# Scan products of two units in one TensorE run, and decays masked by GpSimd selects

## What is computed

```python
xBC = jax.nn.silu(conv)                       # 4 taps over time
dt_p = jax.nn.softplus(dt + dt_bias)
A = -jnp.exp(A_log)
dA = jnp.exp(dt_p * A)
dtx = dt_p[..., None] * x
def step(state, inp):
    dA_t, dtx_t, B_t, C_t = inp
    state = state * dA_t[..., None, None] + dtx_t[..., None] * B_t[:, :, None, :]
    y_t = jnp.einsum('bhpn,bhn->bhp', state, C_t)
    return (state, y_t)
...
yn = (yg * lax.rsqrt(var + EPS)).reshape(B, L, I) * norm_weight
yn = yn * jax.nn.silu(gate)
```

## Time and profile before

| | |
|---|---|
| median of 3 runs | 3058.53 us (3056.78 to 3059.67) |
| profiled execution | 3058.11 us, span 3056.6 us |
| TensorE busy | 3001.3 us, 98% of the span |
| VectorE busy | 2137.6 us, 70% |
| ScalarE busy | 1750.5 us, 57% |
| GpSimd busy | 678.0 us, 22% |
| mean granted TensorE clock | 0.997 |

### The profile page before, as it was taken

One profiled execution on the slowest core, in us unless ns is written; L12 is line 12 of the kernel. 1 busy time (PEld: TensorE's weight loads), 2 busy tenths in 40 slices (PEclk: granted clock), 3 DMA queues, 4 the chain that ended last, 5 costly groups with the idle time before them and its releaser, 6 DMA issues.

```text
span 3056.6 us, 45099 instructions
## 1 busy us (share of the span) xinstructions
PE 3001.3 (98%) x14304; PEld 2339.3 (77%) x14304; DVE 2137.6 (70%) x2660; ACT 1750.5 (57%) x3716; POOL 678.0 (22%) x543
## 2 busy tenths in 40 slices
PE   7999999999999998999999999999999999999998
PEld 6777777777777777777777777777776888887787
DVE  7767666676666676767666666766667878677877
ACT  3576575757566575576665757575665232234443
POOL 3322223121212234312222231212124000001112
PEclk9999999999999999999999999999999999999999
DMA  3434343343425353434243433434254444456665
GB/s 130 165 132 150 104 159 122 137 141 107 158 92 173 104 185 120 157 121 168 98 167 104 157 123 136 140 110 159 92 173 151 145 141 148 144 197 210 212 209 182
DMA packets 125528, 444.86 MB, mean 146 GB/s; under 512 B 17488, under 2 KB 21712, under 8 KB 109008
## 3 DMA queue, kind: packets, MB, share of 16 engines
q1 hardware_dynamic: 117552, 423.14, 41.0%
q0 software_dynamic: 4096, 14.68, 1.2%
q10 hardware_dynamic: 3744, 5.51, 0.5%
HBM read 397.86 MB, written 45.42 MB: 145 GB/s over the span
## 4 chain that ended last, share of the span: by engine, by line
PE 79%; DVE 6%; issue 6%; DMA 3%; POOL 3%; ACT 2%; DVEq 0%; SPq 0%; POOLq 0%; ACTq 0%
PE bank L1077 17%; PE bank L1079 17%; PE bank L1078 17%; PE bank L1115 9%; PE bank L1320 5%; PE bank L1321 5%; PE bank L1322 5%; PE bank L1089 2%; PE bank L1101 2%; DMA acc<-in_w_out 2%; DVE acc L816 1%; PE bank L1125 1%; POOL gate L459 1%; DVE xbc L828 1%; POOL gate L483 1%
## 5 line engine op out<-in xcount | busy, mean ns | idle before, releaser
L1077 PE MATMUL bank<-x_hi,w_hi 128*128 128x512 f32 x2560 | 1020.1, 398 | 1.4 <-DVE acc L816 1.4
L1079 PE MATMUL bank<-x_hi,w_lo 128*128 128x512 f32 x2560 | 999.0, 390 | 0.0
L1078 PE MATMUL bank<-x_lo,w_hi 128*128 128x512 f32 x2560 | 996.7, 389 | 0.0
L816 DVE SCALAR_TENSOR_TENSOR acc<-bank,conv_w,acc 128x511 f32<-128x511 f32 (+2 forms) x576 | 431.0, 748 | 277.7 <-ACT acc L604 248.8
L1077 PEld LDWEIGHTS bank<-x_hi,w_hi 128*128 128x128 f32 x2560 | 480.5, 188 | 114.9 <-issue 21.3
L1079 PEld LDWEIGHTS bank<-x_hi,w_lo 128*128 128x128 f32 x2560 | 480.5, 188 | 103.6
L1078 PEld LDWEIGHTS bank<-x_lo,w_hi 128*128 128x128 f32 x2560 | 481.2, 188 | 94.7
L604 ACT ACTIVATE acc<-bank,tap_par 128x512 f32<-128x512 f32 x192 | 149.6, 779 | 529.1 <-PE bank L1079 498.0
L1320 PE MATMUL bank<-x_hi 128*128 128x512 f32 x1008 | 394.3, 391 | 10.7 <-DVE x_lo L1315 7.0
L1321 PE MATMUL bank<-x_lo,x_hi 128*128 128x512 f32 x1008 | 393.0, 390 | 0.0
L1322 PE MATMUL bank<-x_hi,x_lo 128*128 128x512 f32 x1008 | 392.9, 390 | 0.0
(11 more groups left out here) (162 smaller groups left out, 3393.4 us busy)
## 6 DMA issues: line engine op xcount, KB each, us to landing
units<-cum_scratch SPq DMA_DIRECT2D x128, 1280.0 KB, 6.7
w_raw<-in_w_in SPq DMA_DIRECT2D x160, 512.0 KB, 3.7
w_raw<-y_scratch SPq DMA_DIRECT2D x128, 512.0 KB, 3.7
y_scratch<-gate SPq DMA_DIRECT2D x32, 1024.0 KB, 6.6
acc<-in_w_out SPq DMA_DIRECT2D x128, 256.0 KB, 3.8
xbc<-in_x SPq DMA_DIRECT2D x16, 512.0 KB, 6.3
units<-in_x SPq DMA_DIRECT2D x16, 512.0 KB, 3.7
rstd_b<-rc_scratch SPq DMA_DIRECT2D x32, 256.0 KB, 4.3
```

The costliest lines, as they stand in the source:

```text
L816: dve.scalar_tensor_tensor(acc[:, s % 2, back:], bank_proj[s % 2][:, 0:SEQ - back], mix.conv_w[:, at, m, 3 - back:4 - back], acc[:, s % 2, ...
L1077: pe.matmul(out, w_hi[m % 2][:, k, :], hi, start=(k == 0), stop=False)
L1078: pe.matmul(out, w_hi[m % 2][:, k, :], lo, start=False, stop=False)
L1079: mm = pe.matmul(out, w_lo[m % 2][:, k, :], hi, start=False, stop=(k == KT - 1))
```

## The change

1. The plans place two units' transposes in one slot and two units' products in one slot; in LATER that is slots 11, 15, 19 and 23 for the products (11, 13, 15, ... for single units before). Channel sums of both sequences stand in one slot, and the store and reload of the reciprocal roots, and the rescaling, of both in one slot each.
2. The transposes have two PSUM banks (the second is shared with a part of the scores), the ring of decay buffers has four instead of three.
3. The stored rows hold negated cumulative sums relative to the strip's own block, so that a single Exp covers a whole strip. Above the diagonal a GpSimd select (`hide`, four a unit, 128x256 each) writes 32768 in place of the value, and Exp makes it zero. Four Relu and five Exp of a head become four Exp. `masked` becomes a copy without the mask.
4. For the room, the raw weights and the tanh have one buffer instead of two, with the waits that go with it, and the mask is 256 wide. The table `dec` is gone. In the output phase raw y lies where B and C lay.

```diff
-RING = 3
+RING = 4
...
-LATER = Plan(cb=[5, 7], load=[4, 5, 7, 10, 12, 14, 16, 18], mult=[9, 11, 13, 15, 17, 19, 21, 23],
-             gate_from=CONV_SLOTS)
-LAST = Plan(cb=[5, 7], load=[4, 5, 7, 10, 12, 14, 15, 17], mult=[9, 11, 13, 14, 16, 18, 20, 21],
-            gate_from=CONV_SLOTS, exp=[6, 7, 8, 9, 10, 11, 11, 12, 13, 14, 15, 16, 17, 18, 18, 19])
+LATER = Plan(cb=[4, 6], load=[5, 6, 9, 10, 13, 14, 17, 18],
+             exp=[6, 7, 8, 9, 10, 11, 12, 13, 14, 15, 16, 17, 18, 19, 20, 21],
+             attn=[8, 10, 12, 14, 16, 18, 20, 22], turn=[8, 8, 11, 11, 15, 15, 19, 19],
+             mult=[11, 11, 15, 15, 19, 19, 23, 23], gate_from=CONV_SLOTS, norm_after=3)
+LAST = Plan(cb=[4, 6], load=[5, 6, 8, 9, 12, 13, 15, 16],
+            exp=[6, 7, 8, 9, 9, 10, 11, 12, 13, 13, 14, 15, 16, 16, 17, 18],
+            attn=[8, 10, 11, 13, 15, 16, 18, 19], turn=[8, 8, 11, 11, 14, 14, 17, 17],
+            mult=[11, 11, 14, 14, 17, 17, 20, 20], gate_from=CONV_SLOTS, norm_after=2)
...
+        self.hide = exp[0::2]
-        self.norm = [s + 2 for s in mult[-SEQS:]]
-        self.var = [s + 3 for s in mult[-SEQS:]]
-        self.rc = [s + 4 for s in mult[-SEQS:]]
-        self.rb = [s + 5 for s in mult[-SEQS:]]
-        self.scale = [s + 6 for s in mult[-SEQS:]]
-        self.store = [s + 7 for s in mult[-SEQS:]]
+        self.norm = [s + norm_after for s in mult[-SEQS:]]
+        self.var = [s + 1 for s in self.norm]
+        self.rc = [s + 3 for s in self.norm]
+        self.rb = [s + 3 for s in self.norm]
+        self.scale = [s + 4 for s in self.norm]
+        self.store = [s + 5 + q for q, s in enumerate(self.norm)]
...
         def load_w(g, at, m):
             n = TILES * g + m
-            need(sp, w_split, n - 1)
-            sp.dma_start(w_raw[:, m % 2, :, :], w_tiles[TILES * at + ORDER[m]]).then_inc(w_loaded[m % 2], 16)
+            need(sp, w_split, n)
+            sp.dma_start(w_raw[:, :, :], w_tiles[TILES * at + ORDER[m]]).then_inc(w_loaded, 16)
...
+        def hide(g, u):
+            r = u % RING
+            pool.wait_ge(cum_loaded[r], 16 * (RING_USES[r] * g + u // RING + 1))
+            pool.nop(nofuse=True)
+            for k in range(CHUNKS):
+                near = attn[r][:, :, OFFSET[k]:OFFSET[k] + P]
+                op = pool.affine_select(out=near, in_=near, compare_op=ALU.is_ge, fill=NEVER, base=0,
+                                        pattern=[[0, 2], [1, P]], channel_multiplier=-1)
+            op.then_inc(hidden, 1)
...
         def piece(g, plan, half, s):
+            for u in due(plan.hide, s):
+                hide(g, u)
...
         def tanh(g, s):
             act.wait_ge(conv_taken, CONV_SLOTS * g + s + 1)
-            act.activation(th[:, s % 2, :], acc[:, s % 2, :], ACT.Tanh).then_inc(tanh_done, 1)
+            if s:
+                act.wait_ge(silu_done, CONV_SLOTS * g + s)
+            else:
+                need(act, gate_done, GATE_SLOTS * g)
+            act.activation(th[:, :], acc[:, s % 2, :], ACT.Tanh).then_inc(tanh_done, 1)
...
             if v < 2:
-                act.wait_ge(silu_done, CONV_SLOTS * g + s - 1)
                 need(act, stored[q], 16 * g)
+            if v:
+                act.wait_ge(gate_done, GATE_SLOTS * g + v)
             else:
-                act.wait_ge(gate_done, GATE_SLOTS * g + v - 1)
+                act.wait_ge(silu_done, CONV_SLOTS * (g + 1))
...
-            if h == 0:
-                act.wait_ge(cum_loaded[u % RING], 16 * (RING_USES[u % RING] * g + u // RING + 1))
+            act.wait_ge(hidden, UNITS * g + u + 1)
             for k in range(CHUNKS):
-                part = tile[:, OFFSET[k]:OFFSET[k] + P]
-                op = act.activation(part, part, ACT.Relu, bias=mix.cum[:, CHUNKS * q + k, head], scale=-1.0)
-            op.then_inc(fall_done, 1)
-            for k in range(CHUNKS - 1):
-                part = tile[:, OFFSET[k] + P:OFFSET[k] + WIDTH[k]]
-                act.activation(part, part, ACT.Exp, bias=mix.dec[:, CHUNKS * q + k, head])
...
+                part = tile[:, OFFSET[k]:OFFSET[k] + WIDTH[k]]
+                op = act.activation(part, part, ACT.Exp, bias=mix.falls[:, CHUNKS * q + k, head], scale=-1.0)
...
-        def masked(g, half, q, first):
+        def scores_out(g, half, q, first):
...
-                op = dve.tensor_tensor(bc[:, q, OFFSET[k]:OFFSET[k] + WIDTH[k]], cb_out[k],
-                                       core.mask[:, 0:WIDTH[k]], ALU.mult)
+                op = dve.tensor_copy(bc[:, q, OFFSET[k]:OFFSET[k] + WIDTH[k]], cb_out[k])
...
         def load_small(half):
-            need(sp, multiplied, UNITS * (half * GROUPS - 1) + UNITS - 2)
+            need(sp, multiplied, UNITS * (half * GROUPS - 1) + UNITS - 1)
```

More of the change, by code:

```diff
@@ L50 @@
 LOG_ZERO = -110.0
+NEVER = 32768.0
 def need(eng, sem, value):
@@ L130, in __init__ @@
         self.dt = sb("dt", [P, NT, HEADS])
-        self.cum = sb("cum", [P, NT, HEADS])
-        self.dec = sb("dec", [P, NT, HEADS])
+        self.falls = sb("falls", [P, NT, HEADS])
 class Plan:
-    def __init__(self, cb, load, mult, gate_from, exp=None):
+    def __init__(self, cb, load, exp, attn, turn, mult, gate_from, norm_after):
         self.cb, self.bc = cb, [s + 1 for s in cb]
[L141 to L144, removed]
+        self.load, self.exp, self.attn, self.turn, self.mult = load, exp, attn, turn, mult
+        self.hide = exp[0::2]
@@ L250, in mixer_programs @@
     w_branch = sq[:, :].rearrange("p (k c) -> p k c", c=CW)
-    far = sums[:, 0, 0:3 * SEQS * HEADS].rearrange("p (a q h) -> p a q h", a=3, q=SEQS)
-    cum_hm = bc[0:HEADS, :, :]
-    causal, ones, one = core.mask[:, 0:P], core.mask[:, P:2 * P], core.mask[:, SEQ - 1:SEQ]
+    far = flat(sums)[:, 0:6 * SEQS * HEADS].rearrange("p (q a h) -> p q a h", a=6, q=SEQS)
+    rows_hm = bc[0:HEADS, :, :]
+    causal, ones, one = core.mask[:, 0:P], core.mask[:, P:2 * P], core.mask[:, 2 * P - 1:2 * P]
     d_heads = rstd_b[:, 1, 0:HEADS]
@@ L393, in step @@
                         load_w(g + 1, after(at, plan), ahead - TILES)
-                    elif ahead < TILES + 2:
-                        sp.wait_ge(w_split, TILES * g + ahead - 1)
-                        sp.wait_ge(silu_done, CONV_SLOTS * (g + 1))
-                        output.load(sp, 0, 0, ahead - TILES)
+                if ends_all(half, plan) and s in OUTPUT_LOADS:
+                    sp.wait_ge(cb_done, SEQS * (g + 1))
+                    sp.wait_ge(silu_done, CONV_SLOTS * (g + 1))
+                    output.load(sp, 0, 0, OUTPUT_LOADS.index(s))
                 for group in open_groups(g, s, half, plan, before):
@@ L780, in sums_bank @@
     def sums_bank(half, plan, q):
-        return bank_tr[:, q * CHUNKS:(q + 1) * CHUNKS] if ends_all(half, plan) else bank_y[q][:, 0:CHUNKS]
+        return bank_tr[0][:, q * CHUNKS:(q + 1) * CHUNKS] if ends_all(half, plan) else bank_y[q][:, 0:CHUNKS]
     def variance(dve, g, q, bank):
@@ L886, in piece @@
             for q in due(plan.bc, s):
-                masked(g, half, q, plan is FIRST)
+                scores_out(g, half, q, plan is FIRST)
             for u in due(plan.turn, s):
@@ L1011, in early @@
                 dve.wait_ge(e.cum_copied, 1)
-                dve.tensor_tensor(far[:, 0], cum[:, :, 2, :], tot[:, :, 1, :], ALU.add).then_inc(e.far_step, 1)
-                dve.tensor_tensor(far[:, 1], cum[:, :, 3, :], tot[:, :, 2, :], ALU.add).then_inc(e.far_step, 1)
-                dve.wait_ge(e.far_step, 2)
-                dve.tensor_tensor(far[:, 2], far[:, 1], tot[:, :, 1, :], ALU.add).then_inc(e.far_step, 1)
-                dve.tensor_tensor(mix.dec[:, :, :], by_head(bank_tot[:, :]), mix.cum[:, :, :],
-                                  ALU.subtract).then_inc(e.far_step, 1)
+                for n in range(3):
+                    at = (0, 3, 5)[n]
+                    last = falls[:, :, 1:, :] if n == 0 else far[:, :, at - 3 + n:at, :]
+                    if n:
+                        dve.wait_ge(e.far_step, n)
+                    dve.tensor_tensor(far[:, :, at:at + 3 - n, :], last, tot[:, :, 0:3 - n, :],
+                                      ALU.subtract).then_inc(e.far_step, 1)
             t = s - 2
@@ L1201, in early @@
                 need(pe, e.cum_hm_copied, 3 * q)
-                near = [mix.cum[:, CHUNKS * q + k, :] for k in range(CHUNKS)]
-                ahead = [far[:, a, q, :] for a in range(3)]
-                for i, table in enumerate([near[0], near[1], ahead[0], ahead[2], near[1], near[2], ahead[1],
-                                           near[2], near[3], near[3]]):
+                near = [mix.falls[:, CHUNKS * q + k, :] for k in range(CHUNKS)]
+                ahead = [far[:, q, a, :] for a in range(6)]
+                for i, table in enumerate([near[0], ahead[0], ahead[3], ahead[5], near[1], ahead[1], ahead[4],
+                                           near[2], ahead[2], near[3]]):
```

74 lines of the change are left out of this document (36 added, 38 removed).

## The result

The changed kernel takes 3174.14 us (median of 4 runs, 3173.18 to 3176.51) against 3058.64 of the kernel before: 1.038 times as long, interval 1.037 to 1.040, some 116 us slower. The forecast of 3098 had the direction and a third of the size; the range ended at 3118.

What follows compares the result with a forecast made beforehand. TensorE, busy in 98% of the span, was taken as the bound. Middle groups 12 x (5.4 - 1.7) = +44, ends -3, boundary and tail 0, on 3058.1 us: about 3098, range 3030 to 3118.

Steps and rivals of the forecast that it cites:

- Runs of two units: TensorE's fp32 runs: a second unit behind the first saves 0.3 us a pair, 1.2 for a group's four pairs.
- Selects, 0.4 us each: GpSimd's selects of 128x256 take about 0.4 us, a unit's four 1.6, bounds 1.2 and 2.4.
- Start and length of the rescaling: GpSimd, middle group: starts at 20.0 us after slot 7's start; eight products 11.9 plus 2.6 for unit 1's decay product.
- Chain to slot 14: Middle group: unit 2's select done at 36.1, then 13.9 us of steps; projection 14 starts at 50.0, TensorE waits 5.4.
- Split of the wait: Middle group: of TensorE's 5.4 us wait, about 1 us falls ahead of slot 13.
- Half clock: Rival, TensorE at half clock after each wait: 1.6 us a stretch, up to 20 in all, 3110 to 3118; chance 0.15.
- FIRST and LAST groups: 4 x -1.2, and LAST, whose unit 2 is ahead of the rescaling but unit 3 behind it, waits about 1 us twice: Ends of the halves: each of four groups saves 1.2 us, LAST's waits counted against it; together -3.
- Boundary and tail 0: Half boundary and tail: small weights waiting for unit 6's product and an earlier last transpose count 0, within 3 us either way.
- One weight buffer: Next tile's load starts after VectorE's split of the present one, ScalarE wants it two slots on; given nothing of its own.
- selects in time: Rival: unit 2's select is done before 30.7, so only the runs count, -25 us: 3033; chance 0.25.
- half-way: Rival: no engine exclusion in the rescaling, select done near 33, wait about 2.3 us, +4: 3062; chance 0.13.

Runs made afterwards that it cites:

- experiment 3: Changed kernel without the GpSimd selects and without their place in the queue, Exp waiting for the load itself: 3082.86 us, ratio 1.008 to the kernel before.
- experiment 1: Changed kernel with LATER's loads of units 0 to 3 earlier and the selects of units 2 and 3 ahead of the rescaling: 3105.46 us, ratio 1.016.
- 5: Changed kernel with selects of 4 columns a head instead of 128, in the same places of GpSimd's queue: 3169.34 us, ratio 1.037.
- experiment 6: Changed kernel with FIRST's transposes, decay products and products by single units, its loads and Exps moved to suit: 3154.65 us.
- 9: The eighth kernel with LAST by single units too, selects of units 0 to 3 ahead of the rescaling: 3059.08 us, ratio 1.000.
- experiment 10: As 9, and in FIRST SyncE issues an even slot's weight load ahead of the branch tile's load: 3050.12 us, ratio 0.997.
- eighth kernel: Changed kernel with selects of units 2 and 3 early in LATER and LAST, FIRST by single units, small weights in unit 4's buffer: 3079.63 us, ratio 1.008.

## Why the prediction fell short, point by point

- **Runs of two units**: right. 32 products in 4.53, and a middle group without waits 1.7 shorter (experiment 3).
- **Selects, 0.4 us each**: right, 406 ns at the median, 1.48 for a unit's four.
- **Start and length of the rescaling**: 20.0 and 14.5 forecast, 21.2 (563.25 - 542.05) and 14.47 measured. The decay product fell into it, as said, and stretched to 3.91. Eight products at 1.29, the weight split at 1.23 and the decay product at 2.82 make 14.4, as if one ran after the other. The Trainium skill ("SBUF — State Buffer", section "Who interferes with whom") has a VectorE instruction with two SBUF inputs and a GpSimd instruction that reads SBUF exclude each other, and the trace agrees: by the prediction the selects of unit 2 end near 36 with that rule and near 33 without, and the trace has 37.1 (577.68 + 1.46 - 542.05).
- **Chain to slot 14**: 50.0 forecast, 51.1 measured (593.15 - 542.05). Its parts after the select sum to 14.0 against 13.9 (the addends as printed give 13.8, and the sum of all terms 3099, not 3098; nothing hangs on either). Experiments 1, 3 and 5 show that the select's place behind the rescaling makes this wait.
- **Split of the wait**: about 1 us ahead of slot 13 was forecast, 2.26 measured.
- **Half clock**: left out of the forecast because of that split. After the wait of 2.26 the clock was granted at 0.50, the 1.2 GHz level (584.27 to 587.51). Such a stretch of 3.4 us came once in each middle group. Where it falls on projection 13 it fills time that slot 14 waits for anyway (1.66 idle there in group 3); where it falls behind slot 14, as in group 4 with waits of 2.16 and 3.14, it costs 1.6 (145.4 us against 143.8). Middle groups come to 144.3 - 139.5 = 4.8 on average where 3.7 was forecast.
- **The step that failed**: the terms for the ends, "FIRST and LAST groups: 4 x -1.2, and LAST, whose unit 2 is ahead of the rescaling but unit 3 behind it, waits about 1 us twice" and "Boundary and tail 0". With the two groups behind FIRST these stretches were forecast at 5 us and cost 67, of which about 10 (twice 4.8) are the ordinary waits of those two groups. The working followed one chain, that of LATER, in the steady state. FIRST got only the saving of the runs: in each half TensorE waited 8 us behind it for decay products (2.56, 4.02, 1.50). LAST's wait was of the right kind and too small: 5.75 us in the first half and 3.81 in the second, each with a stretch at half clock. Replacing the paired plans by single units returns about 20 us in FIRST (experiment 6) and 21 in LAST (9).
- **What in the paired plans costs** is only in part known. A pair brings two squares with one buffer, two gate products and two decay products into few slots, and the weight split and the convolutions stand behind. But LATER has the same pairs and, with its selects early, no wait above 0.6 us (experiment 1). Its pairs stand four slots apart, with their squares in even slots behind that slot's weight split. FIRST's stand two or three slots apart, and two of its pairs have their squares in slots 19 and 21, right ahead of a split. No run separates the pairs from their spacing and place, since experiments 6 and 9 replaced whole plans.
- **One weight buffer, "nothing of its own"**: no split waits for its weights in the middle group above, but in FIRST one does. There the load stands on SyncE behind a branch tile's. The kernel before has that order too, but two buffers, and waits 1.28 us at that place against 4.40. With the order changed FIRST's two groups are 7 us shorter (experiment 10).
- **The rivals**: the selects were not in time (experiment 1 shows the kernel that "selects in time" described: a middle group at 138.2; it takes 3105 and not 3033, since the same ends are missing from that sum too), and "half-way" is excluded by the stretched rescaling.

Step by step from 3174 to 3050, each step read from medians of different chips (the kernel before moved by up to 2 us between them): 69 by the selects' place in LATER, 26 by the eighth kernel's other moves, 21 by LAST, 9 by the loads.

## What to carry to other kernels

Follow a change through every plan it touches, the ends of the loop too: twelve steady groups, forecast to about 1 us each, hid four ends that cost more. Where two steps are put into one slot, list all that the pair brings along on the other engines (here squares with one buffer, sums, gate products), how far the next pair is, and what stands behind it in order. To test whether an instruction's work or its place in a queue costs, make it small but leave it an instruction of the engine, and move it; a bare wait does not hold the place.

## What the runs showed of the hardware

- A wait-only instruction on GpSimd's queue completed while eight products issued ahead of it had 9.8 us still to run (553.23 against 562.99).
- A gate product of 128x512 on GpSimd took 1.29 us alone; two took 6.06 beside VectorE's decay product. A select of 128x256 took 396 ns to 2.99 us.
- Eight selects on 128x8 took 1.25 us, eight on 128x256 2.91.
